# Unread TensorE products ahead of and among the first batch's scores, and three router terms moved behind attention

## The chip, the cores and the metric

The kernel runs on one core of one Trainium2 chip. The metric is the time of one execution on the device in microseconds (us), lower is better. A core has five engines with their own instruction streams: TensorE (PE, its weight loads PEld), VectorE (DVE), ScalarE (ACT), GpSimd (POOL) and SyncE (SP, which here only issues transfers). They wait for one another through semaphores, and each runs its own stream strictly in the order in which it was written.

## The reference, cut to what matters

Sixteen batches of 128 tokens with 512 features pass a cross attention and then a block of experts:

```python
x = x + jnp.tanh(g_xattn[0]) * _L0_xattn_ref(_layernorm(x), ctx_2048, ctx_2048)
x = x + jnp.tanh(g_ffn[0]) * _L0_ffn_ref(_layernorm(x), ...)
# attention, 8 heads:   qk = einsum('bdm,bdn->bmn', qh, kh) * scale; ret = einsum('bmn,bcn->bcm', softmax(qk), vh)
# experts:   router_logits = x @ w_router; top 4 of 16; silu(x @ w_gate[e]) * (x @ w_up[e]) @ w_down[e]
#            plus a shared expert of 1408 features with a sigmoid gate x @ w_sh_expert_gate
```

The heads are cut out of the 128 tokens (16 tokens a head) and the attention runs over the 512 features, so each head's scores are 512 x 512.

## The kernel before, in words

**Two blocks.** The program has two blocks in a row, `gated_block`'s (attention) and `experts`. Each block ends with a barrier (line 977 in the trace) at which every engine drains its stream and waits for the others.

**Attention.** A batch is done as two groups of four heads, so there are 32 groups (g = 0 to 31), and a loop body, `slot`, for each. Queries and keys are kept as an upper part in the fast matmul type and a lower part, and the parts are written to DRAM and read back as stacks (`q_stack`, `k_stack`) whose 48 rows hold the three products of the parts. `scores(i, g, r, u, half)` (line 808) makes one half of a unit of plain scores into `score_ps`; two halves, in the two halves of the array's rows, make one unit, and a group has eight. DVE reduces each unit to maxima (`unit`, line 701). A unit waits until DVE has reduced the unit two before it, since there are two pairs of banks. When a group's eight units are reduced, POOL splits the maxima (`split_maxima`, lines 540 and 542), PE turns them together with the values (`values_and_maxima`, lines 854 and 856), ACT copies them out (line 618) and the rows are stored into `q_stack`. Then the transposed scores can be made with the maximum already subtracted (`scores_t`, step T, line 835), ACT takes exponentials (line 652, sixteen a group), and `by_values` (steps B to E, line 846) multiplies by the values into `o_ps`.

**The order on PE** is written out by hand: in front of the slots stand the eight units of g = 0, two of g = 1, `values_and_maxima` of g = 0 and two more units of g = 1. Slot 0 follows `FIRST_ORDER`, the other slots `ORDER`; S is a half of a unit, T one transposed score, C, D, E and B the four quarters of `by_values`, M `values_and_maxima`. In slot g the units of g + 1 and g + 2 are made.

```python
FIRST_ORDER = "SSSSTTSSTSSTSSTSSTCTTOMTTSSSTSTDSTTSLSTTSE"
...
elif u == 2:
    pe.wait_ge(max_done, n)
```

**The start.** SP loads the rows of batches 0 and 1, stores their parts, loads the stacks 0, 1 and 2, waits for the maximum rows of g = 0 (`max_rows[0]`), loads stack 3 and then the rows of batch 2 (line 361). On DVE the statistics of batch 2 (`statistics`, line 682) stand between unit 7 of g = 1 and unit 0 of g = 2. `places` holds `q_hi` and `k_hi`, the upper parts, which ACT writes at lines 580 and 585. PE's first wait is for nine constants that POOL sets (the last are at line 503).

**The end of attention.** After the last group, PE makes the router's logits of batches 0 to 14 out of eight terms (`part_of_router(n)`, line 914; each term is four matmuls of 32 output rows side by side, and each of these is two instructions in the trace). Five terms stand ahead of the turning of the last batch's normed rows (`normed_t`, line 875) and three behind it. DVE makes the last batch's rows (line 771), their statistics and the normed rows `yn` (line 779); ACT and DVE split the turned rows (lines 673 and 783). SP's `keep_y` copies `x_res` into `y_all` (line 410, SBUF to SBUF) and stores `yn` in DRAM (line 411), and waits for both.

**The start of the experts.** PE's `router` makes the logits of the last batch (line 1590, sixteen short instructions) into the last 32 by 128 of the same bank and signals `router_done`. Meanwhile ACT, DVE, DVE, ACT and DVE in turn make the hidden rows of the first chunk (lines 1263, 1472, 1478, 1267, 1485), whose first products were made in attention. PE's `down` (line 1635) waits for these; in its middle it turns the logits (`turn_logits`, line 1599) which ACT has copied (line 1270, behind the upper hidden part in ACT's order), DVE keeps them (line 1346, behind the second tile's lines 1472 and 1478), and the next first products (line 139, from 440.72 us on) wait for that.

Of the kernel before, what the change touches and what calls it, by code (L numbers as in the profile page):

```python
# [23 lines left out]
F32 = mybir.dt.float32  # L24
# [6 lines left out]
P = 128  # L31
# [113 lines left out]
def gated_block(nc, x, ctx_in, g_xattn, g_ffn, w_router, w_gate, w_up, w_down, ws_gate, ws_up, ws_down, w_eg, out):  # L145
    B, TOK, D = x.shape
# [15 lines left out]
    with ExitStack() as whole:  # L162
# [108 lines left out]
        def batch_late(s):  # L271

            return 2 * s.r - 1 if s.q == 1 else 2 * s.r
# [82 lines left out]
        def _(sp):  # L356
# [50 lines left out]
            def keep_y(b, j, done, n):  # L407

                sp.wait_ge(done, n)
                sp.dma_start(y_all[:, bass.ds(b * D, D)], x_res[j][:, :]).then_inc(y_kept[j], 16)  # L410
                sp.dma_start(yn_dram[b], yn[:, :]).then_inc(yn_stored, 16)
# [28 lines left out]

            slots(sp, slot)
            keep_y(B - 2, 0, yn_done, B - 1)
            keep_y(B - 1, 1, last_yn, 1)
            for j in range(2):
                sp.wait_ge(y_kept[j], 16 * (B // 2))
            sp.wait_ge(yn_stored, 16 * B)


# [229 lines left out]
        def _(dve):  # L678
# [34 lines left out]
                dve.tensor_tensor(dst, view[:, :, :, 0:HD], recip[:, :, :, :].to_broadcast([P, KC, HG, HD]),  # L713
                                  ALU.mult).then_inc(norm_done, 1)

            def last_statistics(b, j, done, n):

                dve.wait_ge(done, n)
                dve.bn_stats(bn2[:, :], x_res[j][:, :]).then_inc(bn2_done, 1)

            def last_variance(b):

# [6 lines left out]
            def slot(s):  # L729
                q, g = s.q, s.g  # L730
                q1, q2 = (q + 1) % 4, (q + 2) % 4
                if s.known() and g == 0:
                    unit(1, 1, 4)
                    unit(1, 1, 5)
                if s.before(NG - 1):
                    unit(q1, g + 1, 6)
                    unit(q1, g + 1, 7)
                if prepared(s):
                    statistics(q // 2, s.r + 1)
                if has_late(s):  # L740
                    last_statistics(batch_late(s), 1 if q == 1 else 0, y_done, batch_late(s) + 1)
                if s.before(NG - 2):
                    unit(q2, g + 2, 0)
                if prepared(s):
                    dve.wait_ge(bn_done, 2 * s.r + q // 2 + 3)
                    dve.sem_inc(dve_waited, 1)
                    first_variance(2 * s.r + q // 2 + 2, q // 2)
                if has_late(s):
                    dve.wait_ge(bn2_done, batch_late(s) + 1)
                    dve.sem_inc(dve_waited, 1)  # L750
                    last_variance(batch_late(s))
                if s.before(NG - 2):
                    unit(q2, g + 2, 1)
                if s.at_least(1):
                    normalise((q - 1) % 4, g - 1, batch_of_previous(s), bank_of_outputs(s))
                if s.before(NG - 2):
                    for u in range(2, 6):
                        unit(q2, g + 2, u)
# [4 lines left out]
            for u in range(4):  # L763
# [4 lines left out]
            dve.wait_ge(s_tanh, 1)  # L768
            dve.wait_ge(back_done, B)
            dve.wait_ge(res_loaded[1], 16 * (B // 2))  # L770
            dve.scalar_tensor_tensor(out=x_res[1][:, :], in0=sb_ps[:, 1, :], scalar=tanh_g[:, 0:1], in1=x_res[1][:, :],
                                     op0=ALU.mult, op1=ALU.add).then_inc(last_y, 1)
            last_statistics(B - 1, 1, last_y, 1)
            dve.wait_ge(bn2_done, B)
            last_variance(B - 1)
            dve.wait_ge(rstd2_done, B)
            dve.wait_ge(ynt_done, B - 1)
            dve.wait_ge(yn_stored, 16 * (B - 1))
            dve.tensor_scalar(yn[:, :], x_res[1][:, :], mean_var2[:, 0:1], rstd2[:, 0:1],
                              ALU.subtract, ALU.mult).then_inc(last_yn, 1)  # L780
            at = slice((B - 1) * TOK, B * TOK)
            dve.wait_ge(last_hi, 1)
# [5 lines left out]
        def _(pe):  # L788
# [128 lines left out]
            def slot(s):  # L917
                q, g = s.q, s.g
                halves = [(unit, n_th) for unit in units_of(s) for n_th in range(2)]
                order = LAST_ORDERS[g - NG + 2] if s.known() and g >= NG - 2 else FIRST_ORDER if s.known() and g == 0 else ORDER  # L920
                e = 0
                for step in order:
                    if step == "T":
                        scores_t(s, e // HG, e % HG)
                        e += 1
                    elif step == "S":
                        unit, n_th = halves.pop(0)
                        scores(*unit, n_th)
                    elif step in "CDE":
                        by_values(q, g, "CDE".index(step))  # L930
                    elif step == "B" and s.at_least(1):
                        by_values((q - 1) % 4, g - 1, KC - 1)
                    elif step == "O" and s.at_least(1):
                        if s.before(NG - 2):
                            pe.wait_ge(max_done, 8 * g + 17)
                        else:
                            pe.wait_ge(max_done, 8 * NG)
                            pe.wait_ge(norm_done, g - 1)
                        outputs_t(g - 1, bank_of_outputs(s))
                    elif step == "F":  # L940
                        part_of_products()
                    elif step == "M" and s.before(NG - 1):
                        pe.wait_ge(exp_done, 16 * g + VALUES - 2)
                        values_and_maxima((q + 1) % 4, g + 1, 2 * s.r + (q + 1) // 2, VALUES % 3)
                    elif step == "L" and (has_back(s) or has_late(s)):
                        pe.wait_ge(exp_done, 16 * g + score_at(s, place_of_turned(s) - 3) + 1)
                        if has_back(s):
                            turn_back(batch_back(s), bank_of_turned(s))
                        if has_late(s):
                            normed_t(batch_late(s), bank_of_turned(s), yn_done, batch_late(s) + 1)  # L950

            for u in range(8):
                for half in range(2):
                    scores(0, 0, 0, u, half)
            for u in range(2):
                for half in range(2):
                    scores(1, 1, 0, u, half)
            values_and_maxima(0, 0, 0, LAST % 3)
            for u in range(2, 4):
                for half in range(2):  # L960
                    scores(1, 1, 0, u, half)
            pe.wait_ge(o_cleared, 1)
            slots(pe, slot)
            by_values(3, NG - 1, KC - 1)
# [6 lines left out]
                part_of_router(n)  # L971
            pe.wait_ge(yn32_done, B - 1)
            normed_t(B - 1, LAST % 3, last_yn, 1)
            for n in range(5, 8):
                part_of_router(n)

        attn.close()
        experts(nc, whole, sem, ex, y_all, yn_dram, ident, w_r, tanh_g, out, o_ps)
# [2 lines left out]
def experts(nc, whole, sem, ex, y_all, yn_dram, ident, w_r, tanh_g, out, logits_ps):  # L981
# [592 lines left out]
    def _(pe):  # L1574
# [11 lines left out]

        def router():

            for n, (a, k) in enumerate((a, k) for a in range(2) for k in range(KC)):
                mm = pe.matmul(d_ps[3][3 * 32:4 * 32, SPAN - TOK:SPAN], w_r[:, k, :],  # L1590
                               ex.yn_t[:, a, k, (B - 1) * TOK:B * TOK].bitcast(F32), start=(n == 0), stop=(n == 2 * KC - 1))
            mm.then_inc(router_done, 1)
# [184 lines left out]
```

## Time and profile before

| | us |
|---|---|
| median of three runs | 1150.39 (1148.1 to 1153.3) |
| the profiled execution | 1152.54 |
| its span, from the first to the last instruction | 1150.8 |
| attention block, to the barrier | 433.8 |
| mean granted TensorE clock over the span | 0.998 |

| engine | busy us | share |
|---|---|---|
| PE | 1117.6 | 97% |
| DVE | 814.8 | 71% |
| POOL | 605.8 | 53% |
| ACT | 524.6 | 46% |

The busy time of PE counts a matmul from its start to a modelled end, with neighbours overlapping, so a PE that is busy all the time need not be at its best pace. The views used below are the page itself, the timeline (instructions in order of time, merged; in brackets how long the engine sat idle before and what released it), the groups of instructions by shape over a stretch, the windows (busy time of each engine in a stretch, the granted clock and the DMA share), the transfers by line with their time to landing, and the instructions of one line.

### The profile page before, as it was taken

The page shows a single profiled execution, that of the slowest core. Times are in us where ns is not written, and L with a number is a line of the kernel's source. Part 1 is how long each engine was busy: PE and PEld are TensorE (multiplying, and loading weights), DVE is VectorE, ACT ScalarE, POOL GpSimd, SP SyncE. Part 2 cuts the span into 40 slices and gives each one's busy share as a digit, 9 for nine tenths or more (in the row PEclk, how much of TensorE's full clock was granted, in tenths as well). Part 3 has the DMA queues.
Part 4 walks back from the last instruction along what each step waited for, and adds up shares of the span by engine and source line. Part 5 has one row for each costly group of instructions (what it writes and reads, how often), then busy time and mean ns, then how long its engine had stood idle before and what let it go on. Part 6 is the DMA issues. An engine that isn't in the chain of part 4 may idle for free.

```text
span 1150.8 us, 21590 instructions
## 1 busy us (share of the span) xinstructions
PE 1117.6 (97%) x5718; PEld 745.4 (65%) x5719; DVE 814.8 (71%) x1162; ACT 524.6 (46%) x1055; POOL 605.8 (53%) x597
## 2 busy tenths in 40 slices
PE   3999999999999999999999999999999999999998
PEld 1344444444444447887888878887788888778887
DVE  6799999989998517664443566666667666547977
ACT  1688888888888741111111144444444444321111
POOL 3246555565554324037667357466664756238762
PEclk9999999999999999999999999999999999999999
DMA  9567777877777109955454355666657566433665
GB/s 238 157 186 199 226 193 194 206 207 212 187 201 196 44 23 352 394 168 206 158 208 155 133 156 170 213 187 198 203 177 225 182 201 200 146 98 106 181 187 189
DMA packets 138943, 214.59 MB, mean 186 GB/s; under 512 B 16144, under 2 KB 61712, under 8 KB 138896
## 3 DMA queue, kind: packets, MB, share of 16 engines
q1 hardware_dynamic: 108124, 131.36, 39.4%
q0 software_dynamic: 18016, 61.88, 16.7%
q10 hardware_dynamic: 12756, 20.77, 5.4%
q8 instruction: 25, 0.41, 0.2%
q14 instruction: 22, 0.18, 0.0%
HBM read 117.48 MB, written 91.75 MB: 182 GB/s over the span
## 4 chain that ended last, share of the span: by engine, by line
PE 46%; POOL 9%; DMA 5%; issue 1%; DVE 1%; ACT 0%; SPq 0%; POOLq 0%; DVEq 0%; ACTq 0%
PE score_ps L139 20%; PE score_ps L1676 9%; PE d_ps L1635 8%; POOL w_split L1174 6%; PE d_ps L1700 5%; DMA w_raw<-in_L_ffn_w_down_dram 5%; PE o_ps L1635 3%; POOL w_split L1172 2%; DMA stage<-xs_dram 1%; POOL w_raw L123 1%; PE d_ps L1690 0%; PE o_ps L1690 0%; SPq L1137 0%; DVE score_ps L1528 0%; POOLq L1240 0%
## 5 line engine op out<-in xcount | busy, mean ns | idle before, releaser
L701 DVE TENSOR_REDUCE maxima<-score_ps 128x2 f32<-128x1024 f32 x256 | 305.3, 1218 | 33.9 <-PE score_ps L808 32.2
L652 ACT ACTIVATE probs<-sb_ps 128x512 f32<-128x512 f32 x512 | 271.2, 602 | 73.1 <-PE sb_ps L835 72.9
L139 PE MATMUL score_ps<-yn_t,w_split 128*128 128x512 f32 x1056 | 254.6, 397 | 0.0
L1676 PE MATMUL score_ps<-w_split,x_split 128*128 x948 | 248.6, 400 | 2.8 <-POOL w_split L1174 2.6
L139 PEld LDWEIGHTS score_ps<-yn_t,w_split 128*128 128x128 f32 x1056 | 197.0, 188 | 51.3 <-issue 5.1
L1676 PEld LDWEIGHTS score_ps<-w_split,x_split 128*128 128x128 f32 x948 | 172.4, 189 | 37.7 <-issue 5.5
L835 PE MATMUL sb_ps<-q_stack,places 50*128 50x512 f32 x512 | 183.3, 470 | 1.1 <-ACT probs L652 0.4
L808 PE MATMUL score_ps<-places,q_stack 48*128 48x512 f32 x512 | 158.4, 476 | 20.3 <-DMA q_stack<-q_dram 16.2
L1172 POOL CAST w_split<-w_raw 128x1024 fp32r<-128x1024 f32 x63 | 67.3, 1069 | 181.7 <-DMA w_raw<-in_L_ffn_w_down_dram 85.7
L1174 POOL TENSOR_TENSOR w_split<-w_raw,w_split 128x1024 fp32r<-128x1024 f32 x63 | 152.3, 2417 | 5.1
L846 PE MATMUL o_ps<-probs,v_t 128*17 128x512 f32 x1024 | 136.5, 605 | 0.6
L808 PEld LDWEIGHTS score_ps<-places,q_stack 48*128 48x128 f32 x512 | 65.8, 192 | 101.3 <-issue 51.0
L835 PEld LDWEIGHTS sb_ps<-q_stack,places 50*128 50x128 f32 x512 | 77.9, 187 | 81.2 <-ACT probs L652 68.5
L1700 PE MATMUL d_ps<-w_split,h_rows 128*128 x474 | 121.6, 392 | 2.4 <-DVE h_rows L1549 2.4
L1199 POOL DMA_INDIRECT ring<-res_dram,pos x64 | 73.6, 1150 | 61.9 <-DMA res_dram<-stage 38.3
L1700 PEld LDWEIGHTS d_ps<-w_split,h_rows 128*128 128x128 f32 x474 | 88.9, 188 | 22.4 <-issue 4.0
L1267 ACT ACTIVATE h_split<-hid 128x512 fp32r<-128x512 f32 x44 | 27.8, 632 | 151.9 <-DVE hid L1478 141.5
L1635 PE MATMUL d_ps<-w_split,h_split 128*128 128x512 f32 x396 | 94.5, 391 | 1.6 <-DVE h_split L1485 1.6
L1528 DVE STREAM_TRANSPOSE score_ps<-stage 128x512 f32<-128x512 f32 x79 | 88.2, 1118 | 9.1 <-DMA stage<-xs_dram 8.9
L1263 ACT ACTIVATE th<-score_ps 128x512 f32<-128x512 f32 x44 | 26.1, 593 | 134.7 <-PE score_ps L139 100.0
L1288 ACT ACTIVATE stage<-d_ps 128x512 f32<-128x512 f32 x79 | 47.2, 598 | 88.1 <-PE d_ps L1700 86.6
L1190 POOL DMA_INDIRECT xs_dram<-stage,pos x64 | 63.4, 990 | 44.7 <-issue 25.2
(151 smaller groups left out, 1203.1 us busy)
## 6 DMA issues: line engine op xcount, KB each, us to landing
xs_dram<-zero SPq DMA_DIRECT2D x1, 20224.0 KB, 58.7
stage<-xs_dram SPq DMA_DIRECT2D x316, 64.0 KB, 2.2
res_dram<-stage ACTq DMA_DIRECT2D x79, 256.0 KB, 2.4
places<-k_dram SPq DMA_DIRECT2D x64, 192.0 KB, 3.6
q_stack<-q_dram SPq DMA_DIRECT2D x64, 192.0 KB, 4.0
k_dram<-places SPq DMA_DIRECT2D x16, 512.0 KB, 2.9
q_dram<-places SPq DMA_DIRECT2D x16, 512.0 KB, 3.9
w_raw<-in_L_ffn_w_gate_dram POOLq DMA_DIRECT2D x16, 512.0 KB
```

The lines of the kernel that those rows point to most:

```text
L139: mm = pe.matmul(dst[i], w[:, k, f * P:(f + 1) * P], self.yn_t[:, b, k, t * self.SPAN:(t + 1) * self.SPAN], start=(k == 0 and n == 0), sto ...
L652: act.activation(probs[:, c % 2, head(j)[2], :], sb_ps[:, bank_of_score(s, e), :], ACT.Exp, scale=SCALE).then_inc(exp_done, 1)
L701: dve.tensor_reduce(maxima[q % 2][:, :].rearrange("p (h u) -> p u h", u=8)[:, u, :], sa_ps[:, pair_of_unit(q, g, u), :, :], AX_X, ALU.max) ...
L808: mm = pe.matmul(sa_ps[:, pair, hf, :], q_stack[i][rows, u // 4, at:at + P], k_stack[i][rows, u // 4, :], start=True, stop=True)
L835: pe.matmul(sb_ps[:, bank_of_score(s, e), :], k_stack[s.q][rows, p, c * P:(c + 1) * P], q_stack[s.q][rows, p, :], start=True, stop=True).t ...
L846: mm = pe.matmul(o_ps[32 * j:32 * j + HD + 1, :], v_t[q % 2][:, c, j, 0:HD + 1], probs[:, c % 2, j, :], start=(c == 0), stop=(c == KC - 1))
L1172: pool.tensor_copy(hi, raw).then_inc(w_hi_done, 1)
L1174: pool.tensor_tensor(lo, raw, hi.bitcast(F32), ALU.subtract).then_inc(w_lo_done, 1)
L1528: dve.transpose(xt_ps[j].rearrange("p (b c i) -> p b c i", b=4, c=KC), x_rows[j][:, :].rearrange("p (b i c) -> p b c i", b=4, c=KC)).then_ ...
L1635: mm = pe.matmul(d_ps[i][:, :], h_split[t % 2][:, a, f, i * P:(i + 1) * P], w[:, f, :], start=(n == 0), stop=(n == 3 * c.tiles - 1))
L1676: mm = pe.matmul(gu_ps[j], x_split[j][:, b, k, :], w_split[:, bass.ds(at + (a * 3 * ex.PIECE + k * 2 * FE), 2 * FE)], start=(n == 0), stop ...
L1700: mm = pe.matmul(o_ps[j][:, :], h_rows[j][:, a, f, :], w_split[:, bass.ds(at + (b * 3 * ex.PIECE + 2 * ex.PIECE + f * D), D)], start=(n == ...
```

## The change

It makes three edits. First, `keep_clock(n)` makes n products of `q_hi[0]` and `k_hi[0]` (128 x 128 by 128 x 512, one instruction each) into the first bank of `sb_ps`, which nobody reads: 16 before the first scores, one behind each unit of g = 0 and each of the first two units of g = 1, two behind each of the next two, and two in slot 0 (ahead of the third and the fifth step), 32 in all. Before them PE waits for the two upper parts. Second, the last three router terms leave the attention block and stand at the head of `router` in the experts. Third, the last batch's rows are written straight into `y_all`, and the copy from `x_res` goes.

```diff
-            keep_y(B - 1, 1, last_yn, 1)
+            sp.wait_ge(last_yn, 1)
+            sp.dma_start(yn_dram[B - 1], yn[:, :]).then_inc(yn_stored, 16)
             for j in range(2):
-                sp.wait_ge(y_kept[j], 16 * (B // 2))
+                sp.wait_ge(y_kept[j], 16 * (B // 2 - j))
...
-            dve.scalar_tensor_tensor(out=x_res[1][:, :], in0=sb_ps[:, 1, :], scalar=tanh_g[:, 0:1], in1=x_res[1][:, :],
+            last_rows = y_all[:, (B - 1) * D:B * D]
+            dve.scalar_tensor_tensor(out=last_rows, in0=sb_ps[:, 1, :], scalar=tanh_g[:, 0:1], in1=x_res[1][:, :],
...
-                for step in order:
+                for at, step in enumerate(order):
+                    if s.known() and g == 0 and at in (2, 4):
+                        keep_clock(1)
...
+            def keep_clock(n):
+
+                for _ in range(n):
+                    pe.matmul(sb_ps[:, 0, :], q_hi[0][:, 0:P], k_hi[0], start=True, stop=True)
+
+            pe.wait_ge(k_hi_done, 1)
+            pe.wait_ge(q_hi_done, 1)
+            keep_clock(16)
             for u in range(8):
                 for half in range(2):
                     scores(0, 0, 0, u, half)
+                keep_clock(1)
             for u in range(2):
                 for half in range(2):
                     scores(1, 1, 0, u, half)
+                keep_clock(1)
             values_and_maxima(0, 0, 0, LAST % 3)
             for u in range(2, 4):
                 for half in range(2):
                     scores(1, 1, 0, u, half)
+                keep_clock(2)
...
             normed_t(B - 1, LAST % 3, last_yn, 1)
-            for n in range(5, 8):
-                part_of_router(n)
...
         def router():
 
+            for n in range(5, 8):
+                a, k = n // KC, n % KC
+                for t in range(4):
+                    width = SPAN if t < 3 else SPAN - TOK
+                    pe.matmul(d_ps[3][32 * t:32 * t + 32, 0:width], w_r[:, k, :],
+                              ex.yn_t[:, a, k, SPAN * t:SPAN * t + width].bitcast(F32), start=False, stop=(n == 7))
```

## Rows read from the trace of the kernel before

**Rows 1.** The page, part 4: the chain that ended last, by engine.
```profile
PE 46%; POOL 9%; DMA 5%; issue 1%; DVE 1%; ACT 0%; SPq 0%; POOLq 0%; DVEq 0%; ACTq 0%
```
**Rows 2.** Timeline of the start: start us, length us, what, xcount, idle before.
```profile
8.01 0.17 POOL L503 MEMSET v_t<- 128x16 f32 x2
...
16.18 1.22 PE L808 MATMUL score_ps<-places,q_stack 48*128 48x512 f32 x4 [16.18 <-DMA q_stack<-q_dram]
...
17.01 18.40 DVE L701 TENSOR_REDUCE maxima<-score_ps 128x2 f32<-128x1024 f32 x16 [1.77 <-PE score_ps L808]
```
**Rows 3.** PE groups by shape, 15 to 32 us, then 50 to 100: busy us, mean ns.
```profile
L808 PE MATMUL score_ps<-places,q_stack 48*128 48x512 f32 x28 | 11.1, 776 | 20.3 <-DMA q_stack<-q_dram 16.2 <-DVE maxima L701 4.1
...
L808 PE MATMUL score_ps<-places,q_stack 48*128 48x512 f32 x68 | 20.1, 450 | 0.0
```
**Rows 4.** Timeline, from the first maxima to batch 2's statistics.
```profile
26.98 0.37 PE L854 MATMUL sb_ps<-ident,max_parts 128*32 128x128 f32 x1
...
33.44 0.38 SPq L361 DMA_DIRECT2D y_all<-in_x_dram  x1
...
38.13 0.69 DVE L682 BATCH_NORM_STATS2 bn<-y_all 128x6 f32<-128x512 f32 x1 [2.71 <-DMA y_all<-in_x_dram]
```
**Rows 5.** Timeline, second half of slot 0.
```profile
41.20 1.22 PE L808 MATMUL score_ps<-places,q_stack 48*128 48x512 f32 x3
...
42.04 2.36 DVE L701 TENSOR_REDUCE maxima<-score_ps 128x2 f32<-128x1024 f32 x2 [0.89 <-PE score_ps L808]
...
42.78 1.90 PE L846 MATMUL o_ps<-probs,v_t 128*17 128x512 f32 x8
...
45.41 1.23 DVE L701 TENSOR_REDUCE maxima<-score_ps 128x2 f32<-128x1024 f32 x1 [1.02 <-PE score_ps L808]
...
46.72 1.05 PE L846 MATMUL o_ps<-probs,v_t 128*17 128x512 f32 x8
```
**Rows 6.** Timeline of POOL: the splits of the maxima of groups 2 and 3.
```profile
50.79 0.20 POOL L540 CAST max_parts<-maxima 128x16 fp32r<-128x16 f32 x1 [4.37 <-DVE maxima L701]
...
62.46 0.20 POOL L540 CAST max_parts<-maxima 128x16 fp32r<-128x16 f32 x1 [11.17 <-DVE maxima L701]
```
**Rows 7.** Windows: stretch, length, busy PE, PEld, DVE, ACT, POOL, PEclk, DMA share, GB/s.
```profile
41.00:44.50 3.50, 3.50 (x15) 0.99 (x14) 2.50 (x3) 1.94 (x4) 2.99 (x5) 1.00 0.44 165
...
994.00:995.00 1.00, 0.05 (x1) 0.00 (x0) 0.37 (x1) 0.00 (x0) 0.00 (x0) 1.00 0.18 60
...
997.00:998.00 1.00, 1.00 (x4) 0.74 (x3) 0.96 (x4) 0.00 (x0) 0.00 (x0) 0.50 0.46 133
...
1001.00:1002.00 1.00, 1.00 (x6) 0.79 (x5) 0.55 (x2) 0.54 (x1) 0.00 (x0) 1.00 0.69 260
```
**Rows 8.** Timeline of the end of attention.
```profile
430.00 0.55 SPq L410 DMA_DIRECT2D y_all<-x_res  x1
...
430.59 0.59 SPq L411 DMA_DIRECT2D yn_dram<-yn  x1
...
430.76 2.77 PE L914 MATMUL o_ps<-yn_t,w_r 128*32 128x512 f32 x24
...
431.50 0.69 DVE L783 TENSOR_TENSOR yn_t<-sb_ps,yn_t 128x512 fp32r<-128x512 f32 x1 [1.53 <-ACT yn_t L673]
```
**Rows 9.** Transfers issued from 425 to 436 us: KB each, us to landing.
```profile
yn_dram<-yn SPq DMA_DIRECT2D x1, 256.0 KB, 2.5
```
**Rows 10.** The instructions of line 977, the barrier: two drains, ns min/median/max, start.
```profile
L977 PEldq DRAIN  x1: 2758/2758/2758, 430.8 to 430.8; - x1
...
L977 SPq DRAIN  x1: 7/7/7, 433.4 to 433.4; - x1
```
**Rows 11.** Timeline of the start of the experts.
```profile
433.88 1.91 PE L1590 MATMUL o_ps<-yn_t,w_r 128*32 128x128 f32 x16 [0.34 <-PEq L977]
...
437.43 1.63 PE L1635 MATMUL d_ps<-w_split,h_split 128*128 128x512 f32 x6 [1.64 <-DVE h_split L1485]
...
440.72 5.76 PE L139 MATMUL score_ps<-yn_t,w_split 128*128 128x512 f32 x24
```

More of the change, by code:

```diff
@@ L714, in normalise, with last_statistics @@
                                   ALU.mult).then_inc(norm_done, 1)
-            def last_statistics(b, j, done, n):
+            def last_statistics(b, rows, done, n):
                 dve.wait_ge(done, n)
-                dve.bn_stats(bn2[:, :], x_res[j][:, :]).then_inc(bn2_done, 1)
+                dve.bn_stats(bn2[:, :], rows).then_inc(bn2_done, 1)
             def last_variance(b):
@@ L740, in slot @@
                 if has_late(s):
-                    last_statistics(batch_late(s), 1 if q == 1 else 0, y_done, batch_late(s) + 1)
+                    last_statistics(batch_late(s), x_res[1 if q == 1 else 0][:, :], y_done, batch_late(s) + 1)
                 if s.before(NG - 2):
@@ L770, in _ @@
             dve.wait_ge(res_loaded[1], 16 * (B // 2))
-            dve.scalar_tensor_tensor(out=x_res[1][:, :], in0=sb_ps[:, 1, :], scalar=tanh_g[:, 0:1], in1=x_res[1][:, :],
+            last_rows = y_all[:, (B - 1) * D:B * D]
+            dve.scalar_tensor_tensor(out=last_rows, in0=sb_ps[:, 1, :], scalar=tanh_g[:, 0:1], in1=x_res[1][:, :],
                                      op0=ALU.mult, op1=ALU.add).then_inc(last_y, 1)
-            last_statistics(B - 1, 1, last_y, 1)
+            last_statistics(B - 1, last_rows, last_y, 1)
             dve.wait_ge(bn2_done, B)
@@ L778, in _ @@
             dve.wait_ge(yn_stored, 16 * (B - 1))
-            dve.tensor_scalar(yn[:, :], x_res[1][:, :], mean_var2[:, 0:1], rstd2[:, 0:1],
+            dve.tensor_scalar(yn[:, :], last_rows, mean_var2[:, 0:1], rstd2[:, 0:1],
                               ALU.subtract, ALU.mult).then_inc(last_yn, 1)
```

## The prediction, made before the changed kernel was run

> **What bounds the kernel now.** I read the chain of the page first. It puts 46% of the span on PE and about 15% on POOL and the transfers [rows 1]; what is missing from its 100% is the attention block, which the barrier hides from it. Every later wait starts from that barrier, and both the PE-paced and the POOL-paced stretches behind it start over from it, so a microsecond won before the barrier should stay won. The question is therefore only: how much earlier does PE start the first `down` of the experts (437.43 us now)? All three edits lie before that point. I then read the timelines of 0 to 60 us and of 420 to 445 us, instruction by instruction.
>
> At the start PE waits for the first stack until 16.18 us, and then DVE is the bound: sixteen reductions follow each other from 17.01 us for 18.40 us, one every 1.15 us, with no gap to speak of [rows 2]. PE's pair of halves fits inside. The reader should see that PE is slow here but not late. Its half of a unit takes 776 ns, against 450 ns later on [rows 3], and the same eight products by values take 1.90 us at 42.78 and 1.05 us at 46.72 [rows 5]. So until about 44.6 us TensorE runs at the lower of its two levels (1.2 GHz, then 2.4). The clock column prints 1.00 for that stretch all the same [rows 7]; the durations, not the column, carry this argument. From slot 1 on the groups follow each other every 11.67 us [rows 6], PE being dense.
>
> **The 16 products in front.** They can start when the constants are there, at 8.2 us [rows 2]. At the low level a 512-column product should take what the array needs for one of four equal passes of `by_values`, 1.90 / 4, so up to 0.48 us, and 0.26 at the high level [rows 5] (both with their fill). Sixteen take 4 to 7.6 us and end by 15.8 at the latest; the stack lands at 16.18, so PE's wait covers them: cost nothing, and 0.2 to 0.5 us if the stack came a little sooner.
>
> **Those among the units.** Each stands behind a pair, and the next pair waits for a reduction, 1.15 us apart. A pair at the low level streams for about half a microsecond and a product for another half: 1.0 of 1.15 us, so even without any rise in clock DVE stays the bound. Two places are tighter. `values_and_maxima` of g = 0 now stands behind a product; the split maxima are there at about 26.9 and PE starts at 26.98 [rows 4], while unit 1 of g = 1 and the product behind it are through at 26.7 (high level) or 27.2 (low level): 0 or 0.2 us later. The product ahead of the first T is in front of a wait for the maximum rows: 0 to 0.3 us, but that T does not bound, because DVE's order does. I take 0, with 0.3 as the end.
>
> **What a high clock gives at the start.** If the level rises during the 16 products and stays: (a) the first pair is done in 0.50 instead of 0.83 us [rows 2], less the 0.33 between the two means of [rows 3], and the whole row of reductions moves by 0.3 us. (b) The turning of maxima and values takes 1.0 us now, five small products (the first 0.37 [rows 4]), and would take about 0.65 by the ratio of rows 3; the maximum rows, SP's fourth stack and the load of batch 2 behind them move with it: 0.3 us. That load is issued at 33.44 and DVE sits idle for it, 2.71 us, until 38.13 [rows 4]; this wait is a transfer, and no clock shortens it. Everything that PE saves between 31 and 38 us is lost in it. (c) From 41.2 us on PE is the one that DVE waits for. With high-level durations: the unit at 41.20 is reduced from 41.7 instead of 42.04; `by_values` D takes 1.05 instead of 1.90 [rows 5]; so the next unit is reduced from 44.2 (when DVE is free and PE through) instead of 45.41 [rows 5], the fifth from 45.5, the sixth and seventh from 46.8, ending at 49.2 instead of 50.6. That is 1.4 us on the split at 50.79 [rows 6]. Sum of a, b and c: 2.0 us, which slots 1 to 31 carry unchanged, as their period is 11.67 us with everything on the high level already.
>
> Does it stay? The trace has one fall: PE is idle from 994.05 to 996.17 after dense work, the column falls to 0.50 and is back at 1.00 by 1001, with dense products in between [rows 7]. The 16 products at the low level are dense work for longer than that, so I take it that they raise it, and they then end at about 14. But then PE is idle until 16.18, about as long as before the fall at 996, and works with gaps from there to 31 us. Against that, each unit now has three products instead of two. The rows do not decide; I give staying somewhat more than half.
>
> The Trainium skill (TensorE: Matmul & The Clock Gate, Part 1) says of the warm-up that its penalty is under 1% of a typical kernel's span, which speaks against a large gain; by it alone the gain could be anything up to 11.5 us. Here 28 us pass at the low level and cost by my count 0.2%, since DVE and a transfer bound most of them.
>
> **The end of attention.** Now PE sets the barrier: it starts the three terms at 430.76 [rows 8], and its drain ends at 430.8 + 2.76 = 433.56 [rows 10]. SP is just ahead: its second transfer is issued at 430.59 and lands 2.5 us later, 433.1 [rows 8, 9] and its drain stands at 433.4 [rows 10]. With both edits PE is through at 430.9, DVE at 431.50 + 0.69 = 432.2, and SP, which issues the only transfer at 430.00, has it landed at 432.5 or a little sooner, as no copy goes beside it, with 0.3 for the drain. So SP sets the barrier at about 432.75 in place of 433.56: 0.8 us gained. Its ends are 0.15 (the landing does not get shorter and the issue not earlier) and 1.3 (DVE sets it). The Trainium skill (DMA: Bandwidth & Descriptors, the fixed cost) puts a transfer's fixed part at about 2 us, most of it the receipt of the write; by that the landing could be at 432.0 and DVE would set the barrier, a gain of 1.3 us; the measured 2.5 for this very store decides.
>
> **The start of the experts.** The three terms, 2.67 us, now come ahead of the 1.91 us of line 1590, while ACT and DVE make the hidden rows. The cover for them is PE's idle 1.64 us in front of `down` [rows 11]. They overfill it by 1.0. So `down` starts at 437.43 - 0.8 + 1.0 = 437.6: a loss of 0.2, from a gain of 0.3 to a loss of 0.9 with the ends above. What is late next: ACT copies the logits only when line 1590 is through, at 437.6, and only then takes the second tile; DVE, which takes two steps of 0.7 us on that tile first, keeps the logits from 440.2 to 440.6, just before PE needs them at about 440.8 (440.72 now) [rows 11]. Covered, with 0.2 to spare. The copy into `y_all` and `x_res` cost DVE nothing either way: the instruction only writes elsewhere.
>
> **The sum.** 2.0 - 0.2 = 1.8 us less than the profiled execution's 1152.54, so 1150.7; on the median of the runs, 1150.39, which lies 2.2 below, it is 1148.6.
>
> **The rivals.**
> 1. *The clock falls again* in the idle 2.2 us before the first stack or in the sparse stretch after it, and slot 0 is as slow as before. For: the fall after the idle time at 994 to 996 [rows 7]; the present stretch from 31 to 44 us, in which PE has nearly no gaps and the level still stays low to its end. Against: the products raise the work per unit by half. Then at most (a) is left, less 0.2 for a late `values_and_maxima`, less 0.2 at the end: about 0, 1150.4 (1150.0 to 1151.0). A half case, in which it falls and is back by 41 us, keeps (c): 1149.2.
> 2. *Slower:* the barrier does not move, because the store of `yn` with its receipt, not PE, is what SP waits for, and the three terms then stand fully on the path between the barrier and `down`. Place: SP's last wait; price 1.0 - 0.15 = 0.9 us; it decides if the lone store lands later than 433.0. Together with a fallen clock: 1151.3. For: SP's drain ends within 0.2 us of PE's. Against: the store is issued 0.6 us earlier.
> 3. *The edits do not do what they say:* the level does not rise at all from the 16 products, as they have 128 columns of one stationary block only. Nothing in the trace makes a product of this kind count less than others; time as in rival 1.
>
> **How the numbers follow.** The forecast (1148.6) has 0.50, the half case 0.12, rivals 1 and 3 together 0.26, rival 2 0.07, and 0.05 are for what I have not seen, on either side. Every case lies within 2 us of the time before, while 0.5% is 5.75 us, about what a measurement of this kernel can tell from no change; the three runs of before alone spread over 5.2 us. So the chance of no change is high, and the rest is spread of the runs plus the unseen: faster 0.06, same 0.91, slower 0.03. The range takes the cases, 1148.3 to 1151.3, and about 1.5 us on either side for the medians' own spread, a little more below since the sum has its ends there too: 1146.0 to 1152.3.
>
> **What would show it right or wrong.** In the changed trace: a half of a unit at line 808 at about 450 ns between 16 and 31 us (clock stayed) or 776 (fell); the first eight products by values at 36 us in 1.05 or 1.90 us; the split of group 2 at 48.8 or 50.8; the period still 11.67; DVE still idle for batch 2's rows; the barrier about 0.8 us sooner after `yn` than now, set by SP; no idle time ahead of `down`, which starts about 1.8 us sooner in the span than now. The prediction is wrong if the later stretches, which I take as merely shifted, change their own length by more than a microsecond, or if DVE's reductions turn out slower beside a busier PE.

## The result, and the profile after

The changed kernel takes 1153.54 us (median of 20 runs, 1149.45 to 1159.13 without one disturbed run) against 1150.64 us for the kernel before (20 runs on the same chips). The ratio is 1.0030, with a 95% interval of 1.0018 to 1.0042. The forecast was 1148.6 us with a range up to 1152.3, so the sign was wrong and the time lies above the range; that the change stays within 0.5% was right.

The profiled execution of the changed kernel took 1159.09 us (span 1157.3), which is near the top of its own runs. The 6.5 us between the two spans therefore overstate the loss, which is 2.9 us between the medians.

First the starts of the splits of the maxima of groups 0 to 3 on POOL in the changed kernel (start us, length us, what, idle before), which answer to [rows 6]; before, the first two stood at 26.34 and 35.58:

```profile
25.98 0.20 POOL L541 CAST max_parts<-maxima 128x16 fp32r<-128x16 f32 x1 [12.73 <-DVE maxima L702]
39.00 0.20 POOL L541 CAST max_parts<-maxima 128x16 fp32r<-128x16 f32 x1 [12.53 <-DVE maxima L702]
55.62 0.20 POOL L541 CAST max_parts<-maxima 128x16 fp32r<-128x16 f32 x1 [8.27 <-DVE maxima L702]
67.73 0.20 POOL L541 CAST max_parts<-maxima 128x16 fp32r<-128x16 f32 x1 [11.62 <-DVE maxima L702]
```

Group 0 is 0.36 us earlier, group 1 3.4 later, group 2 4.8 and group 3 5.3 later. From there the period is as before, and the last normed rows start at 434.80 instead of 429.43. So all that the attention block loses, it loses between 26 and 68 us.

The timeline of PE in the changed kernel shows how (L810 is a pair of halves of a score unit, L959 a product of `keep_clock`):

```profile
8.48 6.01 PE L959 MATMUL sb_ps<-places 128*128 128x512 f32 x16 [8.48 <-POOL v_t L504]
16.12 0.50 PE L810 MATMUL score_ps<-places,q_stack 48*128 48x512 f32 x2 [1.64 <-DMA q_stack<-q_dram]
...
21.33 0.50 PE L810 MATMUL score_ps<-places,q_stack 48*128 48x512 f32 x2 [0.20 <-DVE maxima L702]
21.77 0.50 PE L959 MATMUL sb_ps<-places 128*128 128x512 f32 x1
22.46 0.50 PE L810 MATMUL score_ps<-places,q_stack 48*128 48x512 f32 x2 [0.19 <-DVE maxima L702]
...
25.04 0.80 PE L810 MATMUL score_ps<-places,q_stack 48*128 48x512 f32 x2
25.76 0.79 PE L959 MATMUL sb_ps<-places 128*128 128x512 f32 x1
26.48 0.79 PE L810 MATMUL score_ps<-places,q_stack 48*128 48x512 f32 x2
...
30.44 0.79 PE L810 MATMUL score_ps<-places,q_stack 48*128 48x512 f32 x2
31.17 1.22 PE L959 MATMUL sb_ps<-places 128*128 128x512 f32 x2
32.32 0.79 PE L810 MATMUL score_ps<-places,q_stack 48*128 48x512 f32 x2
```

At the high level a pair follows a product by 0.69 us only because it waits for DVE; units are 1.13 us apart (21.33, 22.46). At the low level the idle time is gone and units are 1.44 us apart (25.04, 26.48): pair and product take 0.72 each. PE has become the bound. Where two products stand behind a pair, the step from one pair to the next is 1.88 us (30.44, 32.32), so the second product adds only 0.44: a product costs more beside a pair than beside its like. The windows of the same kernel (stretch, length, busy PE, granted clock, DMA share, GB/s) say when:

```profile
20.00:22.00 2.00, 1.60 (x7) 1.00 1.03 214
22.00:24.00 2.00, 1.67 (x6) 0.80 1.05 407
24.00:30.00 6.00, 6.00 (x18) 0.50 0.77 214
...
50.00:54.00 4.00, 4.00 (x17) 0.51 0.77 211
54.00:58.00 4.00, 3.82 (x27) 1.00 0.40 75
```

Now that the level falls from high to low, the column records it: 0.50 from about 23 to 54 us. Before, the column said 1.00 at the start though the durations were those of the low level [rows 7]; then the low stretch ended at 44.6.

At the end of attention the lines that answer to [rows 8, 9, 11] are, from the timeline of the changed kernel:

```profile
434.80 0.55 DVE L781 TENSOR_SCALAR yn<-y_all,mean_var,rstd 128x512 f32<-128x512 f32 x1 [0.94 <-POOL rstd L514]
435.37 0.34 SPq L444 DMA_DIRECT2D yn_dram<-yn  x1
...
437.97 2.35 PE L1606 MATMUL o_ps<-yn_t,w_r 128*32 128x512 f32 x21 [1.77 <-PEq L990]
...
441.79 1.66 PE L1654 MATMUL d_ps<-w_split,h_split 128*128 128x512 f32 x6
```

and from its transfers:

```profile
yn_dram<-yn SPq DMA_DIRECT2D x1, 256.0 KB, 2.1
```

From the start of the last normed rows to the first `down` it is 6.99 us, where it was 437.43 - 429.43 = 8.00. This end of the change gains 1.0 us. It leaves the experts 4.4 us late in this profile (441.79 against 437.43). The remaining 2.1 of the 6.5 us in the span come up within the experts, far behind the last edited line. From the first `down` to the end of the span the experts take 713.4 us before and 715.5 after, but between 706.4 and 715.0 in the profiles of the experiments below, so 2 us between two single profiles say nothing of the change. An idle stretch and a fall of the clock near 1000 us, as in [rows 7], are in the profiles of before, of the change and of e2_tail.

### The profile page after: what moved, and what is told of

Read it like the earlier page. It is cut to its first block, busy times and chain, and to the rows that moved or that the text cites. A ratio compares the mean times of both kernels' runs of the same rounds, so it can differ in the third digit from the quotient of the medians.

```text
span 1157.3 us, 21653 instructions
## 1 busy us (share of the span) xinstructions
PE 1131.9 (98%) x5750; PEld 754.4 (65%) x5751; DVE 817.4 (71%) x1162; ACT 524.7 (45%) x1055; POOL 606.8 (52%) x597
## 4 chain that ended last, share of the span: by engine, by line
PE 48%; POOL 7%; DMA 5%; issue 1%; DVE 1%; SPq 0%; ACT 0%; POOLq 0%; DVEq 0%; ACTq 0%
PE score_ps L139 20%; PE score_ps L1695 11%; PE d_ps L1654 8%; PE d_ps L1719 5%; POOL w_split L1187 4%; DMA w_raw<-in_L_ffn_w_down_dram 3%; PE o_ps L1654 3%; POOL w_split L1185 2%; DMA stage<-xs_dram 2%; POOL w_raw L123 1%; PE d_ps L1709 0%; PE o_ps L1709 0%; SPq L1150 0%; DVE score_ps L1541 0%; PE o_ps L1606 0%
## 5 line engine op out<-in xcount | busy, mean ns | idle before, releaser
L810 PE MATMUL score_ps<-places,q_stack 48*128 48x512 f32 x512 | 158.2, 470 | 3.0 <-DMA q_stack<-q_dram 1.6
L810 PEld LDWEIGHTS score_ps<-places,q_stack 48*128 48x128 f32 x512 | 66.6, 192 | 82.7 <-DVE maxima L702 39.7
L1654 PEld LDWEIGHTS d_ps<-w_split,h_split 128*128 128x128 f32 x396 | 74.2, 188 | 16.2 <-issue 0.2
```

The source lines that it names most:

```text
L810: mm = pe.matmul(sa_ps[:, pair, hf, :], q_stack[i][rows, u // 4, at:at + P], k_stack[i][rows, u // 4, :], start=True, stop=True)
L1654: mm = pe.matmul(d_ps[i][:, :], h_split[t % 2][:, a, f, i * P:(i + 1) * P], w[:, f, :], start=(n == 0), stop=(n == 3 * c.tiles - 1))
```

## The experiments

The theory formed from the profile, **A**: a product among the units is free at the high level and costs at the low one, because pair and product together then take longer than DVE's reduction. Rivals: **B**, the moved router terms lose the time; **C**, something in the expert block does.

**e1_products: the 32 products alone.** The diff is the change's edit to PE's order, nothing else.

> The kernel before with the 32 unread products alone; the three router terms and the copy stay where they were. Theory A (each product behind a unit costs nothing at the high level, but at the low level pair and product take 1.44 us per unit against DVE's 1.13, so PE becomes what the first batch waits for): the start of the last batch's normed rows moves from 429.4 us to 433 to 435, the end of attention gives nothing back, and the median is 3 to 5 us above before, more than the 2.9 us of the whole change. Rival B (the loss is in the moved router terms): 0 to 2 us less than before. Rival C (the loss is in the expert block, by another code layout or clock phase): attention within 1 us of before and still 3 us more in all.

Measured: 1154.4 us, ratio 1.0027 (1.0011 to 1.0043), 3.6 us more than before. Last normed rows at 433.25, units at 1.44 us in its low stretch (the level fell at 20.8 us and rose at 48.1). The products alone lose about as much as the whole change. The last normed rows are 3.8 us late and the median 3.6 us up, so the loss is made in attention and without the moved terms: B and C fall.

**e2_tail: the three terms and the copy alone.**

```diff
+            sp.wait_ge(last_yn, 1)
+            sp.dma_start(yn_dram[B - 1], yn[:, :]).then_inc(yn_stored, 16)
...
-            for n in range(5, 8):
-                part_of_router(n)
```

> The kernel before with the three terms in the experts and without the last copy, no products. Theory A: the distance from the last normed rows (line 779 before) to the first down product shrinks by 1.0 us, from 8.0 to 7.0, all else stays; median 1.0 us less than before (ratio 0.9991). Rival B: this is where the change loses: distance 9 us or more, median 2 to 3 us above before. The prediction on record put it at 0.2 us more than before.

Measured: 1151.41 us beside 1150.76, but the ratio over the rounds is 0.9995 (0.9977 to 1.0012), so the time decides nothing. The profile does: last normed rows at 429.71, first `down` at 436.69, a distance of 6.98 us against 8.00.

**e3_front16: only the 16 products in front.**

> The kernel before with only the 16 products in front. Theory A: TensorE reaches the high level at about 12 us and falls again before 25 us; the units stay bound by DVE at 1.13 us each at either level, so the split of the maxima of group 0 comes at 26.0 instead of 26.3 and the rest is as before: median 0 to 0.5 us less than before. Rival D (raising the level early makes it rise later afterwards, so the front products themselves cost): the first eight products by values still at 1.90 us and the level low until 50 us or later, split of group 2 at 52 or later, median 1 to 3 us more.

Measured: 1150.23 us, ratio 0.9992 (0.9976 to 1.0008). Split of group 0 at 25.86 and of group 1 at 35.12, each 0.5 us sooner than before (26.34 and 35.58), last normed rows at 429.22. The windows of this kernel show that the level was lost as soon as the scores began, and came back at about 45 us, as it did before:

```profile
16.00:20.00 4.00, 2.32 (x8) 0.72 1.21 164
20.00:24.00 4.00, 2.91 (x8) 0.50 1.02 320
40.00:44.00 4.00, 4.00 (x18) 0.50 0.37 134
44.00:48.00 4.00, 3.97 (x21) 0.87 0.84 285
```

So the 16 products cost nothing that shows. DVE's first reduction starts 0.54 us behind the first pair instead of 0.83, which is the gain of the high level, 0.3 us; the other 0.2 is a stack that happened to land sooner (the first pair starts at 16.00, before at 16.18). At the last normed rows 0.2 us of it is left. Rival D falls.

**e4_units_only: the products among the units without the 16 in front.**

> The kernel before with the products among the units and in slot 0, without the 16 in front. Theory A: the whole stretch from 16 us on is at the low level, every one of the first ten units takes 1.44 us instead of 1.13 and the two with double products 1.9, the split of group 0 comes at 28.8 instead of 26.3, and the last batch's normed rows 5 to 6 us later than before; median 4 to 6 us more than before, the worst of the four. Rival E (the level rises during the units because they are denser): by 25 us a half of a unit takes 450 ns, and the median is within 1 us of before.

Measured: 1154.7 us, ratio 1.0033 (1.0017 to 1.0049). Split of group 0 at 28.67, last normed rows at 435.18, 5.75 us late. From the first unit on, the timeline reads as a column of equal steps:

```profile
16.30 0.79 PE L808 MATMUL score_ps<-places,q_stack 48*128 48x512 f32 x2 [16.30 <-DMA q_stack<-q_dram]
17.02 0.79 PE L957 MATMUL sb_ps<-places 128*128 128x512 f32 x1
17.74 0.79 PE L808 MATMUL score_ps<-places,q_stack 48*128 48x512 f32 x2
```

0.72 us for each of the two, so 1.44 for a unit against the 1.15 of [rows 2]. The denser work did not raise the level among the units; E falls, A stands.

**e5_half_rows: the products in the shape of the scores.** A whole product takes 0.72 us beside a pair but adds 0.44 beside another whole product. This asks whether its shape, all 128 rows between halves of 48, is the reason.

```diff
                 for _ in range(n):
-                    pe.matmul(sb_ps[:, 0, :], q_hi[0][:, 0:P], k_hi[0], start=True, stop=True)
+                    for hf in range(2):
+                        rows = slice(64 * hf, 64 * hf + ROWS)
+                        pe.matmul(sb_ps[:, hf, :], q_hi[0][rows, 0:P], k_hi[0][rows, :], start=True, stop=True)
```

> Products alone, as in e1_products, but each one among the units is two products of 48 rows in the two halves of the array's rows, the shape of the scores, with as many columns as before; the 16 in front stay whole. Theory A1 (at the low level a whole-array product and a pair of halves can't overlap at their seams, so each takes 0.72 us where its columns alone would take 0.43): the pairs now follow each other at 0.43 us, a unit with its product takes 0.87 us and DVE's 1.13 is the bound again; split of group 0 at 25.9 to 26.1, of group 1 at 35.1 to 35.6, the last normed rows at 429 to 430, median within 1 us of before. Rival A2 (a product costs 0.72 us whatever its shape): units at 1.44 us at the low level, normed rows at 433 or later, median 3 to 4 us above before, as in e1_products.

Measured: ratio 1.0012 (0.9997 to 1.0027), median 0.8 us above before. The level fell at 20 us, and yet a unit stayed at 1.13 us:

```profile
21.47 0.80 PE L808 MATMUL score_ps<-places,q_stack 48*128 48x512 f32 x2
22.06 0.63 PE L959 MATMUL sb_ps<-places 48*128 48x512 f32 x2
22.60 0.79 PE L808 MATMUL score_ps<-places,q_stack 48*128 48x512 f32 x2
...
28.93 1.04 PE L808 MATMUL score_ps<-places,q_stack 48*128 48x512 f32 x2
...
30.21 1.04 PE L808 MATMUL score_ps<-places,q_stack 48*128 48x512 f32 x2
```

Where the double products leave DVE no share in it, three pairs of halves follow each other in 1.28 us (28.93 to 30.21), 0.43 each. Splits of groups 0 and 1 stand at 26.12 and 36.08, where e1_products had 26.37 and 39.54 at the same level. So of the loss up to group 1, 3.5 of 4.0 us came from whole-array products standing between pairs of halves, and went with their shape. A1 holds for the units. (The half-row products also write to both banks of `sb_ps`, the whole ones only to the first; no run separates this. But whole products follow each other in that one bank without the extra cost.) That the array can't overlap the two shapes is A1's reading of the distances; the runs show the cost, not what goes on inside. The expectation for the end did not hold: the last normed rows came at 431.83, because this execution kept the low level until about 51 us.

**e7_narrow: 128 columns instead of 512 among the units.**

```diff
-                    pe.matmul(sb_ps[:, 0, :], q_hi[0][:, 0:P], k_hi[0], start=True, stop=True)
+                    pe.matmul(sb_ps[:, 0, 0:128], q_hi[0][:, 0:P], k_hi[0][:, 0:128], start=True, stop=True)
```

> Products alone, those among the units 128 columns wide instead of 512, the 16 in front whole. Theory A1: a narrow product at the low level takes 0.11 us of columns and about 0.3 at its seam, so pair and product take 1.1 to 1.15 us and DVE is just the bound: split of group 0 at 26.0 to 26.6, last normed rows at 429 to 430.5. Theory A2: as e1_products, 433.

Measured once: low level from 19 to 46 us, splits at 25.97 and 36.43, last normed rows at 430.27. A quarter of the columns removes most of the loss too, since a unit then takes just the 1.13 us of DVE's reduction; 0.9 us is left at group 1. The cost beside a pair itself stays: the narrow product still starts 0.72 us behind its pair.

**e6_double: twice the products among the units.** This asks whether they keep the level.

```diff
             for u in range(8):
...
-                keep_clock(1)
+                keep_clock(2)
...
-                keep_clock(2)
+                keep_clock(3)
```

> Products alone, two behind each of the first ten units and three behind the next two, 16 in front. If the level stays high (Theory G: the gaps among the units are what lets it fall, and two products close them): a unit takes 1.13 us, the split of group 0 comes at 26.0, of group 2 at 49 to 50, and the last normed rows at 427.5 to 428.5, 1 to 2 us before the kernel before; median 1 to 2 us less. If it falls all the same (Theory A with a fall that density does not prevent): each unit takes 0.72 + 1.15 = 1.87 us at the low level, the last normed rows come at 438 or later, median 6 to 9 us above before, twice the loss of e1_products.

Measured: median 1152.02 us, ratio 1.0026 (0.9999 to 1.0053), in two clusters: nine runs from 1147.34 to 1154.76 with a mean clock of 0.992 to 0.997, three from 1159.58 to 1162.49 with 0.982 to 0.984. The profiled one is of the first kind:

```profile
24.00:32.00 8.00, 8.00 (x35) 1.00 0.64 172
32.00:36.00 4.00, 2.94 (x17) 1.00 0.91 209
36.00:38.00 2.00, 2.00 (x11) 0.63 1.05 307
38.00:50.00 12.00, 11.34 (x45) 0.50 0.62 194
50.00:52.00 2.00, 2.00 (x15) 0.96 1.05 204
```

Each half of the expectation came true in part. In this profile the level survives the units, splits at 26.05 and 35.44, and the mean clocks suggest the same for nine of the twelve runs. But slot 0 has only the two products at its start, PE has gaps from 32 to 36 us, the level falls at 36.5, ahead of the stretch where it was to pay, and stays low until 50 us, later than before. Split of group 2 at 52.13 instead of 50.79.

**e11_hold: the same, with six products in slot 0 instead of two.**

```diff
                 for at, step in enumerate(order):
+                    if s.known() and g == 0 and at in (2, 4, 8, 11, 14, 17):
+                        pe.wait_ge(k_hi_done, 2)
+                        pe.wait_ge(q_hi_done, 2)
+                        pe.matmul(o_ps[:, :], q_hi[1][:, 0:P], k_hi[1], start=True, stop=True)
```

> As e6_double up to slot 0, and six single products in slot 0 as well, behind the pairs up to unit 1 of g = 2, written into o_ps and taken from batch 1's halves. In e6_double the level stayed high through all units and fell at 36.7 us, in the stretch of slot 0 that had no products. Theory G (the gaps let it fall, so filling them carries the level over): the level stays high to the end of slot 0; with DVE, the load of batch 2 and then PE at the high level as the bounds, the split of group 1 comes at 35.3, of group 2 at 49.2 to 49.8 and the last normed rows at 427.5 to 428.3, which is term (c) of the prediction measured: 1.2 to 2 us less than before in the median, with a few runs 8 to 11 us above where it fell early. Rival H (a late rise or a new fall follows whatever is filled): level low again before 42 us, last normed rows at 430 or later, median 0.5 us or more above before.

Measured: median 1150.03 us, ratio 1.0007 (0.9982 to 1.0032, without the longest run), spread from 1145.99 to 1168.62. In the profiled execution the level lasted through 36 to 40 us and fell at 40.5, in the next idle stretch, 1.20 us in which PE waits for DVE, which had itself waited for the rows of batch 2 until 38.04:

```profile
36.00:40.00 4.00, 3.84 (x19) 1.00 0.91 223
40.00:42.00 2.00, 0.89 (x4) 0.62 0.03 8
42.00:50.00 8.00, 8.00 (x32) 0.50 0.70 242
```

Its last normed rows are at 431.22, so rival H describes this execution, though not the median, for which it had 0.5 us or more above before. Two runs with no recorded fall (mean clock 1.000) took 1145.99 and 1147.44 us; two with a low mean clock (0.979 and 0.981), which fits an early fall, 1163.01 and 1168.62. The first two may be the prediction's gain from a level that stays, but no trace shows such a run, runs of before reach 1146.11 too, and in e12_hold_tail one run at 1.000 took 1150.81. What is certain is the risk: two of twelve runs lie 13 us and more above the median.

**e9_terms_only and e10_copy_only: the two parts of the end, one at a time.**

> The kernel before with the three terms in the experts and the copy left in place. If the two parts need each other, SP's second transfer (issued 0.6 us behind the first) now sets the barrier: distance from the last normed rows to the barrier 3.9 to 4.3 us (4.4 before, 3.1 in e2_tail), to the first down product 7.7 to 8.2 us (8.0 before). If the copy didn't matter: 3.1 and 7.0, as in e2_tail.

Measured once: the barrier 4.2 us behind the last normed rows, as expected if SP's second transfer sets it, but `down` 9.7 us behind them, outside both expectations. The timeline and the windows:

```profile
433.82 4.04 PE L1591 MATMUL o_ps<-yn_t,w_r 128*32 128x512 f32 x21 [2.81 <-PEq L975]
...
439.33 1.66 PE L1639 MATMUL d_ps<-w_split,h_split 128*128 128x512 f32 x6
```

```profile
434.00:435.00 1.00, 1.00 (x9) 0.60 0.08 10
435.00:437.00 2.00, 2.00 (x17) 0.50 0.88 249
437.00:438.00 1.00, 1.00 (x15) 0.69 1.07 380
```

PE was idle for 2.81 us, the level fell, and 21 of the 24 instructions of the terms took 4.04 us instead of 2.35.

> The kernel before without the last copy, terms left in attention. PE still sets the barrier: distance from the last normed rows to the barrier 4.4 us and to the first down product 8.0 us, as before. If SP had set it: 0.5 us less.

Measured once: 4.5 and 8.00 us, as before. Taking out the copy alone gives nothing, moving the terms alone loses 1.7 us, both together gain 1.0. In e2_tail and in the changed kernel the idle time was 1.75 and 1.77 us and the level stayed. Each of these is one profile, so together they show that the level can fall at this barrier, not how often.

**e8_front_two_terms: a version meant to beat both.** The 16 products in front, no copy, and terms 6 and 7 in the experts (`range(6, 8)` for `range(5, 8)`).

> A version meant to beat both: the 16 products in front only, the last copy gone, and two of the three router terms in the experts (one stays behind the turned rows). Theory: last normed rows at 429.1 as in e3_front16; from there to the first down product 6.9 to 7.1 us against 8.0 before and 6.99 in e2_tail, since two terms fit the 1.6 us that PE idles there; in all 1.2 to 1.6 us less than before (ratio 0.9987), less than one comparison can tell apart. If PE with one term sets the barrier again: 7.4 us.

Measured: 1149.29 us, ratio 0.9984 (0.9965 to 1.0004). The distance is 6.71 us, and PE is idle for 0.77 us at the barrier and 0.30 ahead of `down`. The last normed rows came at 430.01, 0.9 us later than expected; group 2 was split at 50.91, 0.5 us later than in e3_front16, and the rest of the 0.9 has no experiment.

**e12_hold_tail: e11_hold with this end.**

> e11_hold with the end of e8_front_two_terms (last copy gone, two terms in the experts). Whatever e11_hold does at the start, the distance from the last normed rows to the first down product is 6.7 us, against 8.0 before, and the median lies 1.0 to 1.5 us below that of e11_hold; under Theory G in all 2.5 to 3 us less than before (ratio 0.9976).

Measured: 1148.16 us, ratio 0.9979 (0.9958 to 1.0000, again without the longest run), 1.9 us below e11_hold; the distance is 6.71 us. One of its twelve runs took 1163.38. Of the two I would keep e8_front_two_terms, which has no such run (1147.77 to 1152.78); neither is clear of before by its interval.

## Why the prediction was wrong

**The failed step is the price of a product among the units.** I let a pair stream for half a microsecond and a product for another half, 1.0 of 1.15 us, and concluded that DVE stays the bound "even without any rise in clock". Products of one shape do take that long (0.43 to 0.44 us behind their like at the low level); the seam between a pair in half the rows and a product in all of them, 0.29 us more each time, does not appear in a sum of columns. A unit took 1.44 us, and those with double products 1.88. In the changed kernel that is 3.8 us between the splits of groups 0 and 1 (13.02 us apart, 9.24 before), in e4_units_only 5.75 in all. No row of before showed what follows a pair when the next product has another shape, so the sum rested on a case that I had not looked for.

**Rival 1 came true and was priced at nothing.** The level fell, as I thought possible, at 23 us. I gave that case the time of the kernel before, because I had already declared the products harmless at the low level. Forecast and rival shared the wrong step, so the range did too: its upper end, 1152.3, had no case of more than 0.9 us above before.

**The late rise was not foreseen.** The changed kernel loses 3.4 us up to the split of group 1 and another 1.9 from there to that of group 3: 28.7 us (39.00 to 67.73) against 26.9 (35.58 to 62.46 [rows 6]). All profiles fall into two kinds here. In before, e1_products, e3_front16, e4_units_only, e7_narrow, e8_front_two_terms and the three kernels with an edit at the end only, the level comes back 8 to 11 us behind the split of group 1, and the two groups take 26.4 to 27.5 us. In the changed kernel, e5_half_rows, e6_double, e11_hold and e12_hold_tail it comes back 15 to 17 us behind that split, and they take 28.7 to 29.3. Products among the units are in both kinds (e1_products, e4_units_only and e7_narrow in the first), so what sets the moment stays open. The runs of the changed kernel differ by 10 us among themselves and the longer ones tend to have the lower mean clock (0.988 at 1149.45, 0.982 at 1159.13), which fits such a moment that varies from run to run, but the runs hold no trace to show it.

**What was right at the start.** The 16 products ended at 14.5 us, in the cover of PE's wait for the stack. The quicker first pair gave the 0.3 us that was forecast, in the changed kernel and in e3_front16; the 0.36 and 0.5 at the splits hold a stack that landed 0.06 and 0.18 us sooner. The wait for the rows of batch 2 hardly moved even where the level was high until then: their statistics start at 37.72 us in e6_double and at 38.04 in e11_hold, against 38.13 [rows 4]. The period behind the first groups stayed. Term (c), the 1.4 us of a high level in slot 0, was neither confirmed nor refuted, since in every profile the level was low again from 42 us on at the latest.

**The end of attention was mis-sized in two terms,** with the right mechanism, rival 2 refuted. The store landed in 2.1 us without the copy beside it, not 2.5 (2.0 in e2_tail, and 2.5 again in e9_terms_only, which keeps the copy), and the barrier moved by 1.3 us instead of 0.8. That is the end which I had given to DVE, and DVE is indeed level with SP: its drain ends at 437.6, SP's stands at 437.7. From the barrier to `down` PE took 3.82 us (437.97 to 441.79), where I had added 2.67 and 1.91: the last of the terms and the first of line 1590's short products run side by side. The time from barrier to `down` grew by 0.3 us instead of 1.0. So a gain of 1.0 us, not a loss of 0.2. The Trainium skill (DMA: Bandwidth & Descriptors, the anatomy of one DMA) gives a fixed part of about 2 us for transfers that GpSimd issues, which comes closer to the landing than the 2.5 of the row, in which two transfers shared the engines. This is partly luck: by its formula the 256 KB add 0.6 us, and the whole estimate of 2.6 is above the 2.1 measured. And a cost that stood in no part of the sum was near: with 2.81 us of idle time at that barrier instead of 1.77 the level fell (e9_terms_only).

**The medians.** By their ratios e1_products is 3.1 us above before (1.3 to 4.9) and e2_tail 0.6 below (2.6 below to 1.4 above); the sum, 2.5, and the 3.5 of the change (2.1 to 4.8) agree within these intervals, so the account closes without the expert block. The prediction called itself wrong if the later stretches changed their length by over a microsecond. In the single profiles they did, by 2.1 us, but the profiles of all kernels differ there by up to 9 us.

## What to carry to other kernels

Work added to keep TensorE's level must be priced at the low level, not at the level that it is meant to keep, since the case in which it fails is the case in which it costs: here 3 to 4 us lost for a hoped-for 2. Among matmuls that use half of the array's rows, a product over all rows costs its seams as well as its columns; give filler the shape of its neighbours. When work is moved across a barrier, look at how long TensorE is then idle at it, and move only as much as keeps the gap short: with two of the three terms moved the distance was 6.71 us, with three 6.98, and the idle time 0.77 instead of 1.75.

## What the runs showed of the hardware

The granted clock is recorded only after its first change: before and in e4_units_only the column reads 1.00 from the start, with the same eight products at 1.9 us, while the kernels with products in front show 0.50 for equal durations. The mean clock of a run (0.985 against 1.000) therefore says nothing of which kernel ran longer at the low level.

Raising the level early does not bring its lasting return forward. It was high when the scores began in all kernels with products in front, was lost between 17 and 42 us in all their profiles, and came back between 45 and 54. Without products in front it came back at 44.6 us in before, and at about 50 in e4_units_only (eight products by values take 1.79 us at 48.67 and 1.05 at 52.51). In the changed kernel PE was busy without a gap from 24 to 36 us and again from 40 to 54, and the granted clock was 0.50 all the while. The Trainium skill (TensorE: Matmul & The Clock Gate, Part 1) puts the penalty of the warm-up under 1% of a typical kernel's span; the traces agree so far as no comparison here moved by more than 0.33% either way, but none held the high level through the start, so the whole penalty was not measured.
